# Gated attention with a mixture of experts: shorter grouping, two peels behind the inversion, eight unread products

## The reference

```python
xn = _layernorm(x)
# s: attention with 8 heads of 16; the heads' values are paired
attn = softmax(q @ k.T / sqrt(16))
attn_out = attn @ v[:, :4] - lam * (attn @ v[:, 4:])
s = (0.2 * (_layernorm(attn_out) * ln_w + ln_b)) @ Wo + bo
# g: two experts for each token, of eight
h = mod(int(xn[:, 0] + xn[:, 1]), 8);  sel = {h, mod(h + 1, 8)}
y = sum over e in sel of 0.5 * (relu(xn @ W1[e] + b1[e]) @ W2[e] + b2[e])
g = silu(y)
```

## Time and profile before

| | us |
|---|---|
| median of 3 runs | 412.27 |
| lowest, highest | 411.48, 412.47 |
| the profiled execution | 411.52 |
| its span, first to last instruction | 409.6 |
| busy: TensorE | 381.5 (93%) |
| busy: VectorE | 291.8 (71%) |
| busy: ScalarE | 267.5 (65%) |
| busy: GpSimd | 189.3 (46%) |

### The profile page before, as it was taken

One profiled execution on the slowest core, in us unless ns is written; L12 is line 12 of the kernel. 1 busy time (PEld: TensorE's weight loads), 2 busy tenths in 40 slices (PEclk: granted clock), 3 DMA queues, 4 the chain that ended last, 5 costly groups with the idle time before them and its releaser, 6 DMA issues.

```text
span 409.6 us, 8427 instructions
## 1 busy us (share of the span) xinstructions
PE 381.5 (93%) x2576; PEld 248.3 (61%) x2576; DVE 291.8 (71%) x758; ACT 267.5 (65%) x667; POOL 189.3 (46%) x262
## 2 busy tenths in 40 slices
PE   4996989999999999999999999999999999999993
PEld 2353876565775667766665668765676667764321
DVE  7787996656686757766676767866686767866884
ACT  3581756666765776576666767676766668675783
POOL 7944203454456543565355532663573444541200
PEclk9996999999999999999999999999999999999999
DMA  7975953263216451265105640346136141216740
GB/s 263 343 230 112 242 196 91 80 206 105 79 37 191 111 195 21 79 190 168 46 27 170 189 140 18 136 121 197 48 127 216 22 169 47 81 26 213 230 159 26
DMA packets 36945, 54.75 MB, mean 134 GB/s; under 512 B 6724, under 2 KB 25141, under 8 KB 36903
## 3 DMA queue, kind: packets, MB, share of 16 engines
q1 hardware_dynamic: 31456, 46.94, 34.6%
q0 software_dynamic: 3296, 6.76, 7.8%
q10 hardware_dynamic: 2151, 0.53, 0.6%
HBM read 15.59 MB, written 6.75 MB: 55 GB/s over the span
## 4 chain that ended last, share of the span: by engine, by line
PE 74%; DVE 7%; DMA 5%; ACT 4%; SPq 4%; issue 4%; POOL 1%; ACTq 0%; DVEq 0%; POOLq 0%
PE ring L1393 14%; PE pv_bank L1327 13%; PE ring L1414 12%; PE score L1289 12%; PE exp L1314 10%; PE ring L1251 3%; DVE neg_max L1049 3%; DMA xs<-xn_rows,inverse 3%; SPq L532 2%; PE ring L1335 2%; PE ring L1255 1%; PE ring L1353 1%; PE ring L1276 1%; PE ring L1375 1%; PE score L1264 1%
## 5 line engine op out<-in xcount | busy, mean ns | idle before, releaser
L1049 DVE TENSOR_REDUCE neg_max<-score 128x1 f32<-128x512 f32 x256 | 169.0, 683 | 72.3 <-PE score L1289 66.7
L1289 PE MATMUL score<-ks,qs 96*128 96x512 bf16 x256 | 98.3, 386 | 6.3 <-DVE neg_max L1049 6.0
L787 ACT ACTIVATE probs<-exp 128x512 f32<-128x512 f32 x124 | 72.5, 605 | 36.3 <-PE exp L1314 32.3
L787 ACT ACTIVATE xin<-exp 128x512 f32<-128x512 f32 x120 | 69.7, 604 | 38.5 <-PE exp L1314 38.1
L1314 PE MATMUL exp<-qs,ks 99*128 99x512 bf16 x244 | 91.7, 380 | 0.1
L825 ACT ACTIVATE hT<-ring,pair 128x128 f32<-128x128 f32 x256 | 73.4, 377 | 13.0 <-PE ring L1393 11.9
L1414 PEld LDWEIGHTS ring<-w_sb,hT 128*128 128x128 f32 x568 | 73.5, 191 | 10.4 <-issue 3.5
L1414 PE MATMUL ring<-w_sb,hT 128*128 (+1 forms) x568 | 75.4, 275 | 0.9 <-ACT hT L825 0.9
L1393 PEld LDWEIGHTS ring<-xsT,pair 128*128 128x128 f32 x512 | 66.3, 191 | 14.6 <-issue 8.1
L1393 PE MATMUL ring<-xsT,pair 128*128 128x128 f32 x512 | 68.2, 276 | 1.7 <-issue 1.2
L684 POOL TENSOR_SCALAR tanh<-tanh 128x128 f32<-128x128 f32 x32 | 17.2, 536 | 95.5 <-ACT tanh L845 95.2
(11 more groups left out here) (198 smaller groups left out, 417.4 us busy)
## 6 DMA issues: line engine op xcount, KB each, us to landing
pair<-table SPq DMA_DIRECT2D x32, 580.0 KB
qs<-parts SPq DMA_DIRECT2D x42, 128.0 KB
ks<-parts SPq DMA_DIRECT2D x42, 128.0 KB
xin<-_attn_hidden_states_dram SPq DMA_DIRECT2D x8, 256.0 KB, 4.4
table<-in_L_ffn_W_dram SPq DMA_DIRECT2D x2, 1024.0 KB, 9.2
w_sb<-in_L_ffn_W_dram SPq DMA_DIRECT2D x8, 256.0 KB, 10.4
xn_rows<-xn SPq DMA_DIRECT2D x8, 256.0 KB, 3.0
table<-_attn_hidden_states_dram SPq DMA_DIRECT2D x8, 256.0 KB, 5.4
```

Of the source, the lines that this page charges most:

```text
L787: a.activation(prob(n), exp_banks[n][:, :], ACT.Exp, scale=SCALE).then_inc(exp_done, 1)
L1049: v.tensor_reduce(neg_max[:, b % 2, col:col + 1], score_bank[n % 2][:, :], AX.X, ALU.max, negate=True).then_inc(max_taken, 1)
L1289: t.matmul(score_bank[n % 2][:, :], qs[0:MAX_ROW, b % STK, hh, c * P:(c + 1) * P], ks[0:MAX_ROW, b % STK, hh, :], start=True, stop=True).t ...
```

## The change

It changes times of steps, and seven pieces of code:

- GpSimd's grouping has six groups, with batches 6 and 7 apart. The shift of batches 4 to 7 is computed by GpSimd for all four at once after the last power, ahead of its first norm. VectorE no longer computes a shift; it folds -2 * mean into the sum of the first two features before it waits for the last rstd.
- `count_groups` compares and subtracts on the int32 value directly and keeps h as an integer: four instructions fewer.
- The scan is read one element back (it starts at element 511, a zero), so that it gives the count before each token, and the subtraction behind it is gone.
- The second half of `token` is computed by ScalarE; the inversion waits for two signals.
- `route` 1 stands ahead of the last peel of batch 0 on TensorE; norm 2 ahead of the first evictions on ScalarE.
- peel (1, 0, 2) moves from ahead of the inversion to behind score 1, peel (1, 1, 2) to behind score 5. On ScalarE the eviction of the first then stands behind `load_small`, that of the second behind the first `turn_tile`.
- `keep_busy`: one product of 512 columns, which nobody reads, after each of the scores 2, 3 and 4, and five ahead of score 6. Turn_tile f of the extra tiles stands at t - 3 instead of t - 2.4.
- The three `ones` DMAs are issued by SyncE. On SyncE's queue stack part (0, 1, 2) stands behind the stores of batches 4 to 7, the store of batch 2 ahead of all stack parts.

```diff
-LN_GROUPS = ((0, 1), (1, 2), (2, 4), (4, 6), (6, 8))
+LN_GROUPS = ((0, 1), (1, 2), (2, 4), (4, 6), (6, 7), (7, 8))
-SHIFT_AT = (-58.5, -57.5, -55.5, -53.5, -50)
-NORM_AT = (-58, -56.4, -49.9, -47.93, -49.2, -49.1, -49, -48.95)
+SHIFT_AT = (-58.5, -57.5, -55.5, -53.5, -53.4, -50)
+NORM_AT = (-58, -56.4, -56.3, -47.93, -49.2, -49.1, -49, -48.95)
-QKV_AT = (-57.9, -50, 35, 67, 99, 131, 163, 181)
+QKV_AT = (-57.9, -48.62, 35, 67, 99, 131, 163, 181)
-PEEL_AT = (((-55.5, -55.3), (-55.4, -55.25)), ((-45.5, -45.3), (-45.4, -45.2)))
-STACK_AT = (((-55.58, -55.45, -55.28), (-55.57, -55.35, -55.2)), ((12.1, 12.3, 12.5), (12.2, 12.4, 12.6)))
+PEEL_AT = (((-55.5, -55.3), (-55.4, -48.65)), ((-45.5, 1.5), (-45.4, 5.1)))
+STACK_AT = (((-55.58, -55.45, -55.28), (-55.57, -55.35, -48.64)), ((12.1, 12.3, 12.5), (12.2, 12.4, 12.6)))
-TOKENS_AT = -45
+TOKENS_AT = -45.6
-EXTRAS_AT = 5.2
-GROUPS_AT = (9.05, 10.72, 13.05, 14.05)
+EXTRAS_AT = 4.7
+GROUPS_AT = (9.05, 10.72, 12.55, 14.05)
-TX, DX = 2.4, 3.2
+TX, DX = 3, 3.2
-INIT_AHEAD = 1.5
+INIT_AHEAD = 1.67
-SPLIT_MAX, TURN_MAX = 16.8, 18.9
+SPLIT_MAX, TURN_MAX = 16.5, 18.9
-TANH, GATE = 0.7, 1.84
+TANH, GATE = 1, 1.84
+WARM_AT = ((2.5, 1), (3.5, 1), (4.5, 1), (5.15, 5))
@@ schedule
+    for time, products in WARM_AT:
+        at(time, "keep_busy", products)
@@ sync
+                elif kind == "ones":
+                    (the three DMAs that ScalarE issued)
@@ gpsimd
                     pool.wait_ge(stats_ready, end)
-                    if end < B:
+                    if first not in POOL_NORM:
                         g.tensor_scalar(shift[:, tok], mv[:, tok, 0], -1.0, None, ALU.mult)
...
                 elif kind == "norm" and s[1] in POOL_NORM:
                     b = s[1]
-                    pool.wait_ge(shift_ready, 1 + [b >= end for _, end in LN_GROUPS].index(False))
+                    if b == POOL_NORM[0]:
+                        tok = slice(C * b, NT)
+                        pool.wait_ge(rstd_ready, len(LN_GROUPS))
+                        link(g.tensor_scalar(shift[:, tok], mv[:, tok, 0], -1.0, None, ALU.mult))
+                        link(g.tensor_tensor(shift[:, tok], shift[:, tok], rstd[:, tok], ALU.mult))
@@ scalar
+                elif kind == "tokens":
+                    act.wait_ge(in_tile_ready, 1)
+                    a.activation(token[:, 1, :, :, :], in_tile, ACT.Copy, scale=row_of[:, 0:1]).then_inc(token_ready, 1)
@@ vector, count_groups
+                dve.wait_ge(rstd_ready, len(LN_GROUPS))
                 link(v.tensor_tensor(v01[:, :], v01[:, :], rstd[:, :], ALU.mult))
-                dve.wait_ge(shift_ready, len(LN_GROUPS))
-                link(v.scalar_tensor_tensor(v01[:, :], shift[:, :], 2.0, v01[:, :], ALU.mult, ALU.add))
...
-                link(v.tensor_copy(n_abs[:, :], whole_i))
-                link(v.tensor_tensor(over, n_abs[:, :], v_abs[:, :], ALU.is_gt))
-                link(v.tensor_tensor(n_abs[:, :], n_abs[:, :], over, ALU.subtract))
-                link(v.scalar_tensor_tensor(h[:, :], sign[:, :], -1.0, n_abs[:, :], ALU.add, ALU.mult))
-                link(v.tensor_copy(whole_i, h[:, :]))
-                link(v.tensor_scalar(whole_i, whole_i, EXP - 1, None, ALU.bitwise_and))
-                link(v.tensor_copy(h[:, :], whole_i))
+                link(v.tensor_tensor(over, whole_i, v_abs[:, :], ALU.is_gt))
+                link(v.tensor_tensor(n_abs[:, :], whole_i, over, ALU.subtract))
+                link(v.scalar_tensor_tensor(h_i[:, :], sign[:, :], -1.0, n_abs[:, :], ALU.add, ALU.mult))
+                link(v.tensor_scalar(h_i[:, :], h_i[:, :], EXP - 1, None, ALU.bitwise_and))
...
-                v.tensor_tensor(seen[:, :, :], seen[:, :, :], onehot[:, :, :], ALU.subtract).then_inc(seen_ready, 1)
+                v.tensor_tensor_scan(work[:, 768:1024], work[:, 511:767], zeros,
+                                     0.0, ALU.add, ALU.add).then_inc(seen_ready, 1)
@@ vector, find_tokens
-                v.tensor_scalar(token[:, 1, :, :, :], in_tile, row_of[:, 0:1], None, ALU.mult).then_inc(token_ready, 1)
@@ vector, shift
-                    v.tensor_tensor(v01[:, :], xin[:, :, 0], xin[:, :, 1], ALU.add).then_inc(pair_summed, 1)
-                    dve.wait_ge(rstd_ready, g + 1)
+                    link(v.tensor_tensor(v01[:, :], xin[:, :, 0], xin[:, :, 1], ALU.add))
                     dve.wait_ge(stats_ready, end)
-                    v.scalar_tensor_tensor(shift[:, tok], mv[:, tok, 0], -1.0, rstd[:, tok],
-                                           ALU.mult, ALU.mult).then_inc(shift_ready, 1)
+                    v.scalar_tensor_tensor(v01[:, :], mv[:, :, 0], -2.0, v01[:, :],
+                                           ALU.mult, ALU.add).then_inc(pair_summed, 1)
@@ tensor
+                elif kind == "keep_busy":
+                    for _ in range(s[1]):
+                        t.matmul(exp_bank[1][:, :], qs[0:MAX_ROW, 0, 0, 0:P], ks[0:MAX_ROW, 0, 0, :], start=True, stop=True)
...
                 elif kind == "invert":
-                    pe.wait_ge(token_ready, 1)
+                    pe.wait_ge(token_ready, 2)
```

More of the change, by code:

```diff
@@ L533, in _ @@
                                          parts_of(b)[:, i, k, :]).then_inc(stacked[b % STK], 16)
+                elif kind == "ones":
+                    sp.wait_ge(dve_consts, 1)
+                    for slot_b in range(STK):
+                        sp.dma_start(ks[MAX_ROW:KROWS, slot_b, :, :],
+                                     ones_bf[:, :].unsqueeze(1).to_broadcast([PARTS, HEADS, S])).then_inc(ones_stacked, 16)
                 elif kind == "load_w2":
@@ L727, in _ @@
                     act.dma_start(lnb_sb[:, :], ln_b.rearrange("(p a) -> p a", a=1)).then_inc(small_loaded, 16)
-                elif kind == "ones":
-                    act.wait_ge(dve_consts, 1)
-                    for slot_b in range(STK):
-                        act.dma_start(ks[MAX_ROW:KROWS, slot_b, :, :],
-                                     ones_bf[:, :].unsqueeze(1).to_broadcast([PARTS, HEADS, S])).then_inc(ones_stacked, 16)
                 elif kind == "copy_ninth":
@@ L860, in _ @@
             v.memset(zeros, 0.0)
+            v.memset(work[:, 767:768], 0.0)
             link(v.memset(va[:, :, :, :, HD:VW], 0.0))
@@ L945, in find_tokens @@
                 dve.wait_ge(slots_split, 1)
[L946 to L948 removed]
+                v.tensor_tensor(in_tile, by_pair(slot_tile[:, 0:NT], FT), over_pairs(columns[:, :, :], NT // 2),
+                                ALU.is_equal).then_inc(in_tile_ready, 1)
+                dve.wait_ge(in_tile_ready, 1)
+                v.tensor_tensor(token[:, 0, :, :, :], in_tile, by_pair(ordinal[:, :], FT), ALU.mult).then_inc(token_ready, 1)
             def find_rows(q):
```

15 lines of the change are left out of this document (5 added, 10 removed).

## The result

The changed kernel takes 415.25 us (median of 20 runs, 411.22 to 420.18) against 412.09 us for the kernel before beside it (median of 20, 410.88 to 413.58): ratio 1.0052, 95% interval 1.0032 to 1.0073. The ratio leaves out the four longest runs (418.02 to 420.18), which lie over 1.5% above the shortest. The changed kernel is slower by about half a per cent, where the forecast was no change.

A forecast was written before the change was run, and what follows sets the result against it. VectorE was taken to hold the schedule from 44 to 60 us, so the time of score maximum 8 counted: gain 0.23, minus 0.1 allowed, is 0.13. 411.52 less that gives 411.4 us, range 409.7 to 413.4.

The forecast's parts named there:

- The chain that the working was mostly about: VectorE's routing to the inversion, with ScalarE's new product: `at_row` complete at 27.98, `inverse` 1.08 us earlier.
- Nothing later moved, as forecast: After the front: VectorE holds the pace to 60 us as before; tanh order, bounded 1.4 saved to 0.3 lost, taken as 0.
- the norms' end: GpSimd's norms, which the last `xn` stores follow, end at 26.3 us, bounds 25.5 to 26.9.
- both products in full: Upper bound on GpSimd's norms, 26.9 us: comparison and `token` product (0.81 each) overlap them in full.
- allowed 0.1 us for VectorE's loss: VectorE shut out by GpSimd's norms on the shared port: up to 0.46 at each of two products, 0.1 taken.
- lands, at the 2.1 us minimum: Store 3 on SyncE's queue, issued at 27.5 to 28.2 us, lands at 29.6 to 30.4.
- hidden: Stores landing at 29.6 to 30.4 against `inverse` at 30.1: 0.3 us to spare at one end, not the other.
- the stack part: Stack part (0, 1, 2) behind store 7 on SyncE, about 0.55 us per issue; landing after the inversion would show the forecast wrong.
- C: Rival: port and stores hold the first gather; 0.8 us of the 1.08 lost, 412.2 us; chance 0.13.
- the 35.26 of the working: First gathered row lands at 35.26 us, 1.08 earlier than before the change.
- maximum 8: VectorE's score maximum 8, the one number followed: 39.87 us against 40.10, all behind it shifting with it.
- B: Rival: TensorE's clock falls in or behind the 2.4 us hole; 1.35 to 1.7 us lost, 412.9 us; chance 0.22.

The follow-up runs named there:

- second profile: Another profiled execution of the unchanged changed kernel, run again beside the kernel before on another chip: 416.13 us; that run's median 415.73 us, ratio 1.0106.
- before_spread: Kernel before the change, with load_small's ten DMAs issued one by one between scores 7.7 and 14.45: ratio 0.9972 to the kernel before.
- after_spread: Changed kernel with only load_small's ten DMAs issued one by one between scores 7.7 and 14.45: 411.19 us, ratio 1.0031 to the kernel before.
- peels_only: Kernel before with batch 1's two peels behind the inversion, the eight unread products and extra tiles' turn_tile earlier: ratio 1.0013 to the kernel before.
- no_products: Changed kernel without all eight unread products: median 414.75 us, ratio 1.0081 to the kernel before.
- after_spread_order: Changed kernel, small loads spread out, stack part (0, 1, 2) ahead of stores of batches 4 to 7, store 3 ahead of store 7: ratio 1.0004.
- spread_order_ahead: after_spread_order with the five unread products ahead of the first turn_tile; the fastest kernel: 408.26 us, ratio 0.9936 to the kernel before.

## Why the prediction was wrong

**What held.** The chain that the working was mostly about came as told: the last rstd at 16.81 (17.06), the count ready at 19.47 (19.65), L922 at 20.18 (20.43), the new ScalarE product 1.32 us (1.3), ready at 27.98 (28.0), the inversion done at 29.51 (29.5), `inverse` at 30.06 (30.1). `at_row` was complete at 28.30 (27.98): beside the norms comparison and product took 0.94 each and not 0.81, and three `at_row` 2.51 and not 2.42. Nothing later moved, as forecast: 371.4 us stand behind maximum 8 before and 371.2 after.

**The first step that failed: the norms' end, 26.3 with bounds 25.5 and 26.9; it was 28.62.** The working counted as new overlap the comparison and the `token` product and left out the three `at_row` instructions, which the same change moves 1.45 us forward (27.24 to 25.79), into the norms. The price of an overlap was wrong too: the 807 ns of the earlier trace rows is what one short neighbour does. Against five long two-input instructions back to back, a norm lasted 2.56 us. The bound "both products in full" was no bound.

The page "SBUF — State Buffer" of the Trainium skill, in its section "SBUF: two separate sides", says that the shared pair goes to whichever of the two starts first, for its whole instruction, and that the other fully blocks. The trace agrees on the blocking. It shows more: the norm that began at 25.20 was still running when L955 and the first two `at_row` instructions ended (25.87, 26.74 and 27.60), and ended at 27.76, so GpSimd got no turn at the first two of these ends. The prediction allowed 0.1 us for VectorE's loss by that rule; the large loss was GpSimd's.

**The second: "lands, at the 2.1 us minimum".** Store 3 was issued at 29.63, not at 27.5 to 28.2, and took 6.82 us, 5.52 in the second profile. The earlier trace rows had the median, 3.0, and the longest, 8.1, beside the minimum; the working gives no reason for the minimum. It landed so late because load_small was in flight with it: with the ten loads moved away and nothing else, the same store, issued at 29.75, took 2.3. The working had those ten issues begin "with the last eviction", at about 29.5; ScalarE's queue issues them as soon as it is past its last wait, from 27.24 on, while its activations are still being done. Spread out, they leave the store 2.0 to 2.3 us and the gather 2.5 to 3.0, instead of the 4.7 to 6.1 that it takes when it starts beside them. The gather's 4.89 in the earlier trace rows had been the hint that this costs already before the change: before_spread takes its row at 33.99.

A term was missing here as well. The working set the stores' landing, 29.6 to 30.4, against `inverse` at 30.1 and called the stores hidden. But the gather starts 1.24 us after a store that ends the wait and 0.30 after `inverse`. By these two, its own times give 30.8 to 31.6 for the one and 30.4 for the other: the stores would have held the gather even if they had landed as foretold. So it is in the fastest kernel here, in which the norms are still shut out: in its two profiles the gather starts at 31.96 and 31.80, with `inverse` ready at 30.15 and 30.02.

**The third: the stack part.** The prediction lists stack part (0, 1, 2) behind store 7 and says that a stack part later than the inversion would prove it wrong, but works out only store 3 behind it. By its own 0.55 per issue the part would have been issued between 26.9 and 27.7 us and have landed, at the minimum again, between 29.0 and 29.8, when score 0 was due. It was issued at 29.02 and landed 4.3 us later, beside the small loads; scores 0 and 1, which should have filled TensorE's time from 29.5 on, came at 33.33, at 33.68 in the second profile. There TensorE, at half clock until 37.9, was ready for the row only 0.17 us before it came. So in that execution this step alone makes the row as late as the stores do.

**The rivals.** C (stores hold the gather) named the mechanism and priced it with stores landed by 31.0; they landed at 36.44, and at 35.26 in the second profile. There C is enough by itself: the row comes 4.0 us later than the 35.26 of the working, the clock is full behind it, and the 4.62 us to maximum 8 are the working's 4.61. With 43.88 for 39.87 the prediction's own sum gives 411.4 + 4.0 = 415.4, close to the median of the runs (415.25) and 0.7 under that execution. In the first profile B (the clock falls, five products behind the row) came on top, at 2.64 (maximum 8 came 7.25 us behind the row, not 4.61) where it was priced at 1.35 to 1.7; there 411.4 and the 8.50 by which maximum 8 was late give 419.9, and the execution took 419.59. So 415.25 lies outside of the range because C's size was bounded too low. The clock did fall in both profiles, each time in the first hole, which the working does not have. That C and B are not independent comes second: a later row can be a longer hole, and the prediction gave no chance to the two at once.

**What each part cost**, as far as the runs tell: the five products behind the row 1.04 us in the changed kernel, if it is a difference at all; with the queue in order they take 1.30 us of maximum 8 (39.51 to 38.21), and ahead of the row nothing that shows (409.50 us without them, 408.26 with, intervals that overlap). Queue order and small loads together bring the changed kernel from 1.0052 to 1.0004, load_small alone to 1.0031; these ratios are not from runs side by side, each has an interval of 0.2% either way, and on a second chip the changed kernel itself stood at 1.0106. The grouping's gain of 1.1 us on `inverse` never reached the row in any kernel in which the norms were shut out: they end at 28.6, 3.5 us later than before the change.

## What to carry to other kernels

When an edit makes one engine's chain earlier, list everything of that chain that now overlaps a neighbour on the same port, not only the instructions that the edit touches, and price the neighbour by the whole back-to-back stretch. For every DMA on the path, price the landing by what will be in flight beside it, and write out all that stands behind a delayed entry in an in-order queue. Filler for TensorE's clock belongs ahead of the wait that it is to cover; behind it, it is work on the path (here 1.1 us at full clock and 2.1 at half). Where an engine waits for two things, look at what follows each: here 1.24 us behind the one and 0.30 behind the other.

## What the runs showed of the hardware

- GpSimd's 128x128 norm, 0.45 us alone, lasted 2.56 us beside back-to-back bf16 two-input instructions of VectorE; a 128x1248 one of these went from 0.81 to 0.94. Sixteen norms took 7.9 to 8.0 us without such company and 11.0 with it, the same within 0.04 in ten profiles; 0.9 us in the start of the comparison made 2.6 us in the norms.
- Ten small loads of 0.3 MB in all on ScalarE's queue stretched a 256 KB store from 2.0-2.3 to as much as 6.8 us, a 128 KB stack part from 2.3 to 4.3-4.5, and a gather from 2.5-3.0 to 4.7-6.1.
- An indirect gather on GpSimd that waits for two signals started 1.24 us after the stores' and 0.30 us after the one of `inverse`, whichever came last, in ten profiles each.
- The granted clock went to half in or behind TensorE's holes of 1.81 (after_spread), 2.00 (peels_only, ahead of the inversion), 2.29, 2.56, 2.85 and 3.6 to 4.2 us, and at the start of one of 2.40 (before), each time for 3.4 or 6.8 us; behind one of 2.54 (no_products) it stayed full, as behind 1.59 (after_spread_order) and 0.30 (spread_order_ahead). In before_spread the row left a hole of 0.29 only, but TensorE was busy for 39 to 73% of each microsecond from 30 to 34, and the clock fell at 35.7. What decides between these I can't say.
